# Mixed two-layer kernel: silu and product moved to the head of a pair's slot, seven row transfers moved under the first pairs, first pair one slot earlier

## The reference, cut to what matters

```
xn = layernorm(x);  x = x + hyena(xn) + moe_top4_of_8_plus_shared(xn)     # layer 0
xn = layernorm(x);  x = x + linear_attention(xn) + moe_top2_of_8(xn)      # layer 1
```

```
scores = norm over r of (x @ W_A[e])                  # 8 experts, 2 chosen for each token
y_e    = (silu(x @ W_A[e] @ W_B[e]) * (x @ W_up[e])) @ W_down[e]
out    = sum over the 2 chosen experts of w_e * y_e
```

## Time and profile before

| | us |
|---|---|
| median of 3 runs | 655.79 |
| lowest and highest | 652.28, 659.21 |
| the profiled execution's own time | 649.94 |
| its span, first to last instruction | 648.1 |

### The profile page before, as it was taken

How to read it: one execution, slowest core, us unless ns; L and a number is a source line. 1 busy time by engine, 2 the same in 40 slices (tenths; PEclk the granted TensorE clock), 3 DMA queues, 4 the chain that set the end, 5 groups by cost and what they waited for, 6 DMA issues and landing times.

```text
span 648.1 us, 10568 instructions
## 1 busy us (share of the span) xinstructions
PE 567.0 (87%) x3218; PEld 467.6 (72%) x3218; DVE 447.0 (69%) x1199; ACT 300.8 (46%) x558; POOL 298.2 (46%) x268
## 2 busy tenths in 40 slices
PE   5899999989899998999999999986877877888870
PEld 2879985667687677888888878765665666777660
DVE  6858998729721992344659989987787685656673
ACT  4460247655424441344577657855835433334230
POOL 5610030006561563265334458768344755666661
PEclk9999999999999998999999999997999799999995
DMA  7350031400023502133222232122211232322626
GB/s 215 128 243 17 2 129 33 97 9 2 21 110 110 172 0 65 59 93 94 75 67 79 70 100 79 39 99 68 56 55 59 59 89 71 82 73 67 208 74 223
DMA packets 48381, 54.94 MB, mean 85 GB/s; under 512 B 7029, under 2 KB 40374, under 8 KB 47271
## 3 DMA queue, kind: packets, MB, share of 16 engines
q1 hardware_dynamic: 43542, 42.99, 21.2%
q0 software_dynamic: 4320, 8.99, 4.1%
q10 hardware_dynamic: 466, 2.31, 1.6%
HBM read 36.22 MB, written 15.94 MB: 80 GB/s over the span
## 4 chain that ended last, share of the span: by engine, by line
PE 30%; DVE 12%; issue 9%; ACT 6%; POOL 4%; another core or an unknown queue 4%; DMA 2%; SPq 1%; POOLq 0%; ACTq 0%; DVEq 0%
PE banks L1762 4%; PE banks L1764 4%; PE banks L1763 4%; PE banks L1968 3%; PE banks L1882 2%; PE banks L2119 2%; PE banks L1874 2%; POOL arena L888 1%; PE banks L2104 1%; PE banks L1895 1%; PE banks L1896 1%; DVE arena L1606 1%; DMA arena<-result_rows 1%; PE banks L2075 1%
## 5 line engine op out<-in xcount | busy, mean ns | idle before, releaser
L873 POOL DMA_INDIRECT result_rows<-arena x71 | 69.3, 975 | 38.8 <-PE banks L1764 16.6
L858 POOL DMA_INDIRECT expert_rows<-arena x64 | 63.6, 994 | 40.6 <-issue 14.6
L822 POOL TENSOR_TENSOR arena<-arena 128x512 f32<-128x512 f32 x32 | 40.8, 1275 | 86.2 <-DVE arena L1431 86.2
L888 POOL TENSOR_TENSOR arena<-arena 128x512 f32<-128x512 f32 x32 | 42.4, 1325 | 68.2 <-DVE arena L1585 68.1
L1585 DVE TENSOR_TENSOR arena<-banks,arena 128x512 f32<-128x512 f32 x48 | 33.0, 688 | 42.5 <-PE banks L1764 33.5
L1968 PEld LDWEIGHTS banks<-arena 128*128 128x128 f32 x384 | 48.8, 191 | 6.9 <-POOL arena L888 3.0
L1968 PE MATMUL banks<-arena 128*128 128x128 f32 x384 | 51.6, 277 | 1.9 <-DVE arena L1585 1.1
L1874 PE MATMUL banks<-arena 128*128 128x512 f32 x96 | 50.5, 608 | 2.4 <-DVE arena L1431 1.1
L1882 PEld LDWEIGHTS banks<-arena 128*128 128x128 f32 x256 | 33.0, 191 | 19.0 <-POOL arena L822 14.4
L2119 PE MATMUL banks<-arena 128*128 x284 | 39.6, 284 | 7.4 <-DVE arena L1628 4.0
L1087 ACT ACTIVATE rows_hi<-banks 128x256 fp32r<-128x256 f32 (+1 forms) x36 | 13.6, 379 | 67.7 <-remote 33.6
(11 more groups left out here) (281 smaller groups left out, 1628.7 us busy)
## 6 DMA issues: line engine op xcount, KB each, us to landing
arena<-expert_weights SPq DMA_DIRECT2D x64, 128.0 KB, 3.4
arena<-expert_rows SPq DMA_DIRECT2D x71, 66.0 KB
arena<-in_x SPq DMA_DIRECT2D x8, 512.0 KB, 6.8
arena<-result_rows SPq DMA_DIRECT2D x8, 512.0 KB
arena<-in_dft_f SPq DMA_DIRECT2D x1, 2048.0 KB, 9.6
normed_hi<-xnt_hi SPq DMA_DIRECT2D x1, 2048.0 KB, 6.4
normed_lo<-xnt_lo SPq DMA_DIRECT2D x1, 2048.0 KB, 10.9
arena<-in_dft_i SPq DMA_DIRECT2D x1, 2048.0 KB, 7.7
```

The source lines that it names most:

```text
L822: nc.gpsimd.tensor_tensor(out=T1[:, q % 3, :], in0=T1[:, q % 3, :], in1=T2[:, q % 2, :], op=ALU.add).then_inc(y_in, 1)
L858: pool.indirect_dma_start(out=xrows, out_offset=bass.IndirectOffsetOnAxis(ap=SLOT[:, k, t:t + 1], axis=0), in_=XNF[:, t, :], in_offset=Non ...
L873: pool.indirect_dma_start(out=yrows, out_offset=bass.IndirectOffsetOnAxis(ap=DEST[:, i, n:n + 1], axis=0), in_=YB[:, i % YBUFS, n, :], in_ ...
L888: nc.gpsimd.tensor_tensor(out=AM0[slot % 2], in0=AM0[slot % 2], in1=WB0[:, m, :], op=ALU.mult).then_inc(weighted, 1)
```

## The change

The first pair moves from slot 52 to 51 and the schedule ends one slot earlier. Silu and product come right behind `rows_hi` and `rows_lo`, and `turned` and `result_rows` go to the end of the slot's list. Quarter 2's transfers now stand in slots 43 to 48 (1, 2, 2, 2, 1, 1), with the last seven in slots 51 to 53 (3, 3, 1), each behind its slot's `gate_up`; slots 49 and 50 have none. Quarter 3's stand in slots 56 to 61. Quarter 4's stay in slots 64 to 69. Since PAIR0 has moved, pair 4's rows are turned in slot 54, pair 12's in slot 62 and pair 20's in slot 70. Worked out from `shares()`, slot 68 now has three row and two result transfers (before: three and one).

```diff
-PAIR0 = 52
+PAIR0 = 51
-SCATTER_FROM = (33, 43, 54, 64)
-ROWS_FROM = 55
+SCATTER_FROM = (33, 43, 56, 64)
+ROWS_FROM = PAIR0
-SCATTERS = ((1, 3, 3, 1, 1, 2, 1, 1, 3), (1, 1, 1, 3, 3, 2, 2, 2, 1))
+SCATTERS = ((1, 3, 3, 1, 1, 2, 1, 1, 3), (1, 2, 2, 2, 1, 1))
...
-            rows, results, of_slot = 2 * BT * 2, 0, {}
+            rows, results, of_slot = sum(map(sum, SCATTERS)), 0, {}
...
-                known = 2 * BT * (3 if slot < SCATTER_FROM[3] else 4)
+                known = 2 * BT * sum(slot >= first for first in SCATTER_FROM)
...
-                        if N0 * NCH < slot < PAIR0:
-                            pool.wait_ge(gh_mm, TPC * (NCH - 2) + slot - N0 * NCH)
                         scatter(shares_of[slot - first])
...
@@ ScalarE's slot
                     rows_hi(i + 1)
+                if 0 <= i < NP:
+                    silu_pair(i)
...
                         attention_copy(n)
-                if 0 <= i < NP:
-                    silu_pair(i)
-                if 1 <= i <= NP:
-                    turned(i - 1)
...
                         nc.scalar.activation(e, e, ACT.Exp).then_inc(rt_exp, 1)
+                if 1 <= i <= NP:
+                    turned(i - 1)
...
@@ VectorE's slot
                     rows_lo(i + 1)
+                if 0 <= i < NP:
+                    product(i)
...
-                c = due(slot, 6)
+                c = due(slot, 6 if slot <= N0 * NCH else 5)
...
                 if 0 <= i < NP:
-                    product(i)
                     places_of(i)
-                if 2 <= i < NP + 2:
-                    result_rows(i - 2)
...
                             tables(bt, part)
+                if 2 <= i < NP + 2:
+                    result_rows(i - 2)
```

## The result

The changed kernel takes 667.65 us (median of 5 runs), the kernel before 652.28 in the same measurement (5 runs): a ratio of 1.0225 with an interval of 1.0179 to 1.0271, which is +14.7 us (11.7 to 17.7). The change makes the kernel slower; whether by 2% or more can't be told. The prediction gave 665.6 us with a range of 645 to 679, which is +9.8 us on the 655.79 it started from. Since the kernel before is 3.5 us faster in this measurement, +9.8 is to be held against +14.7, and not 665.6 against 667.65. The profiled execution took 662.47 us, against 649.94: +12.5. It is the fastest of the changed kernel's five runs.

A forecast was written before the change was run, and what follows sets the result against it. TensorE was taken to wait for others in two stretches and nearly bound the attention stage, with pair 20's rows on the path without slack. 5.5 - 4.0 + 1.0 + 7.3 = +9.8 us on 655.79 gave 665.6 us, range 645 to 679.

The forecast's parts named there:

- The wait before pair 3: Up to pair 3's gate_up: TensorE waits for pair 4's rows behind the 32nd transfer; +5.5 us, bounds +3.3 to +8.
- the road: From a quarter's last transfer to rows that can be turned: 7.5 us for pair 4, 7.98 for pair 20.
- Pairs 3 to 12: Slots of these pairs: silu ahead of key features and fewer waits save time, less a lower clock; -4.0 us, bounds -8 to +1.
- The attention slots: Attention stage, 22 pairs: a later attention step is nearly balanced by earlier silus; +1.0 us, bounds -1 to +10.
- a sign against itself: Attention stage: pairs 19 to 31 clearly off 55.8 us would move the cause from transfers to the slots' order.
- Pair 20's rows: Pair 20's turning: one slot earlier while quarter 4's transfers stay, so TensorE waits; +7.3 us, bounds +4.9 to +7.8.
- 5 us or more: Ahead of pair 20's turning: a wait of this length would show the forecast right.
- The edits at nothing: Later places_of, normed_lo at 5 instead of 6 and the removed wait on gh_mm, each taken to cost nothing.
- the rows land before they are wanted: Rival at pairs 4 and 20: their gates never decide, so -9.1 us, 646.7 us; chance 0.30.
- Late completions stay and add: Rival in the attention slots: late signals come on top of the longer chain, +10.8 us more, 676.4 us; chance 0.14.
- The first pair does not start earlier: Rival at pair 0: rows_hi waits to 444.42 as now, so +8.3 in place of +5.5, 668.4 us; chance 0.12.

The follow-up runs named there:

- e9_q3_slot55: The changed kernel with quarter 3's transfers in slots 55 to 60 instead of 56 to 61; ratio 1.0230 to the kernel before.
- e4_q4_by_four: The changed kernel with up to four transfers a slot from slot 64, so quarter 4's sixteen stand in slots 64 to 67; ratio 1.0163 to the kernel before.
- e10_staged_52: The kernel before with only the list order changed, up to pair 11, old order from pair 12, transfers and first pair untouched; ratio 1.0037 to the kernel before.
- e7_both_quarters: The changed kernel with quarter 2's transfers all in slots 43 to 48 and quarter 4's by up to four a slot; ratio 1.0162 to the kernel before.
- e3_q2_early: The changed kernel with quarter 2's transfers back in slots 43 to 51, ungated by gate_up, as in the kernel before; ratio 1.0191 to the kernel before.

## Why the prediction was right

The direction and the main mechanism came out, and the size within a factor of 1.5: +9.8 forecast, +12.5 in the profile and +14.7 by the ratio. Part of it is luck. Pair 3's term was too large and the term behind it too hopeful, and the two errors nearly cancel; and 665.6 lies close to 667.65 because the forecast started from a median 3.5 us above that of this measurement. Its own steps, one by one:

- **The wait before pair 3: right in kind, too large.** +5.5 forecast, +2.2 found in the profile, which is below its bound of 3.3; without the 1.5 us by which this execution was early at the 16th transfer it is +3.7, inside the bound. The chain is as worked out, but `gate_up(0)` came at 439.24, not 441.2 (1.5 of the 2.0 are that chance again), and carried the ranking (446.67 for 448.8) and the 32nd transfer (455.15 for 457.3) with it; and the road from it to usable rows took 6.2 us, not 7.5. The road is not a constant: 6.05 to 6.2 us at pairs 4 and 12, 8.05 at pair 20, where 7.98 stood before.
- **Pairs 3 to 12: the term failed.** -4.0 forecast, -1.15 found. The order's part was right: the two runs that have it without late rows gave -3.9. What failed was the step "`turned` and the features are late instead, in a slot in which pair 12's rows are turned, and I take 0.8 of it", which has those rows there in time. The change moves the pairs one slot ahead and quarter 3 one slot back, which made a third wait of 3.85 us; I had priced pair 20's in full and not this one. `e9_q3_slot55` shows that this shift is its cause: one slot back, and the wait is gone.
- **The attention slots: the sign right, the size off.** +1.0 forecast over 22 pairs. The order's own cost is about 5 us over the last 16 (3.3 in the run of the order alone). The prediction named as a sign against itself that pairs 19 to 31 take clearly more or less than 55.8 us. They took 58.4, and the order does carry that part, though not the most of the loss. The working had the mechanism (TensorE's attention step starts late) but gave slots that gain as much as others lose. Pairs 12 to 18 went 2.95 faster in the profile; the other runs with this order gave 34 to 41 us there, so that gain is no property of the change. It may be part of why the ratio gives 2 us more than the profiles, which I haven't shown.
- **Pair 20's rows: right.** +7.3 forecast, +8.2 found. The last transfer went 2.65 us behind the end of pair 18's `gate_up` (1.95 forecast), and 8.05 us followed (7.98). `e4_q4_by_four` took the wait away and with it 8.8 us of that slot. The wait on the turning itself was 3.53 us, less than the "5 us or more" of the signs, as TensorE had idled 3.94 us in the same slot for the ring of result buffers. That ring stands in no term of the sum. The late rows cover it here, and it decides the runs that bring quarter 2's rows in time.
- **The edits at nothing** were not all nothing: `normed_lo` behind product holds the first down product. In the changed kernel the wait for rows covers this; in the runs without that wait pair 2's slot is longer by 1.1 us (slot 53, where `normed_lo` itself waits for ScalarE) to 3.6 us (`e10_staged_52`, slot 54).

Of the rivals, "the rows land before they are wanted" was wrong as far as its point went: the 32nd transfer went at 455.15, not by 446.5. More than that, when a run made it true the gain did not come in the total (`e7_both_quarters`, +10.5 us), though it came in both stretches; full result buffers and late completions took it behind them. "Late completions stay and add" wasn't the case for the changed kernel, where they fell. Its ground, "every third transfer in a row has gone with one", reads too much into the rows: in the attention stage only eleven of 23 silus were late. "The first pair does not start earlier" was wrong: it started 6.3 us earlier. But what was held against that rival, no transfers in slots 49 and 50, isn't the reason: with transfers there the first pair started just as early behind the 16th transfer (`e3_q2_early`, 27.57 us for 27.54).

From the Trainium skill's fixed cost of about 2 us a transfer ("DMA: Bandwidth & Descriptors", Anatomy of one DMA, SWDGE path) the prediction estimated some 5 us for the road. The page gives that figure for GpSimd's transfers, and the second transfer of the road is a load on SyncE's queue. The traces show 6.05 to 8.05 us, so the estimate is too short for a road with two transfers and a queue between.

## What to carry to other kernels

When a consumer is moved ahead, every producer that it gates on must be counted against it, one by one, by the distance in slots from the last item sent to the first one wanted: here three quarters stood in line. Where the last transfer stood one slot ahead of the turning (quarters 2, 3 and 4 after the change) TensorE waited 7.89, 3.85 and 3.53 us; where it stood two slots ahead, 0.47 us (quarter 4 before) or not at all (quarter 3 in `e9_q3_slot55`). Quarter 4's transfers never moved, and still came late. Work put first in a list puts everything else later, so ask for each later item who waits for it in order; silu and product first gained 3.9 us in one stretch and cost about 5 in another. A repair has side effects of its own, too: the constant that brought quarter 2's rows in time also kept four results back, and some 5 us were lost 13 pairs later. And two traces are to be compared from the last point that the edit can't have touched, not from the start of the span: executions of the same code reached it up to 5 us apart.

## What the runs showed that was not expected

With runs of GpSimd's indirect transfers, TensorE's completion signals reach ScalarE and VectorE late, by 2 us and more (up to 4.97 in the changed kernel). With two instead of three of them in a slot eight slots took 32.9 us instead of 38.1, and the silus' sum of lateness fell from 5.8 to 1.0 us. The profile names such a releaser only as "remote". By what way the transfers delay the signals, the runs don't show.
